# A two-stage conditioned MLP with layer norms: statistics first, GpSimd makes the norm's offset and the second table copies, z's transposes between the halves of a first layer

## The chip, the cores and the metric

The kernel runs on one core of a Trainium2 chip. The metric is the device time of one execution in microseconds; lower is better.

## The reference

Input `x` holds 128 sequences of 64 tokens with 256 features, with two numbers for each sequence: a condition (0, 1 or 2) and a domain (0 to 15).

```python
# stage 0, by condition
out_nr  = gelu(x @ w1_nr  + b1_nr)  @ w2_nr  + b2_nr      # two layers
out_tsr = gelu(x @ w1_tsr + b1_tsr) @ w2_tsr + b2_tsr     # two layers
out_sr  = gelu(gelu(x @ w1_sr + b1_sr) @ w2_sr + b2_sr) @ w3_sr + b3_sr   # three layers, 512 wide first
y = layernorm(x + chosen_out) * gamma + beta
# stage 1, by domain
h = gelu(y @ down_W.T + down_b)                           # 64 wide
h = h @ expert_W[domain].T + expert_b[domain] + domain_emb[domain]
out = layernorm(y + h @ up_W.T + up_b) * ln_gamma + ln_beta
```

All is float32. The gelu is exact.

## The kernel before

**Slots.** The kernel sorts the sequences by condition and packs four of one condition into a slot of 256 tokens: first the three-layer slots (`g < b_sr`), then the two-layer ones. A loop of steps runs over the slots, unrolled by two (parities p = 0 and 1, `q = 1 - p`). The first steps (HEAD) and the last (LAST2, LAST1, LAST0, DRAIN) are written out; the rest (MAIN) is a loop on each engine. Step g works on several slots at once: TensorE makes the last layer of slot g, the first layer of slot g + 1, the transposes of z of slot g - 1 and the expert products of slot g - 2; VectorE finishes slot g - 3.

**Precision.** A float32 product is made of three matmuls, high x high, low x high and high x low. ScalarE makes the high part (`x_hi`, L874; `h_hi`, L888), VectorE the low part of x (`x_lo`, L656), GpSimd the low part of h (`h_lo`, L478, `low()`).

**A two-layer step, engine by engine.** Each engine runs its instructions in the order written, and a wait on a semaphore stops all that stands behind it.

- TensorE: the last layer's products into ps_z (L1131 waits for H1's `h_hi`, then L1136 waits for H1's `h_lo`); the branch L1218; the first layer of the next slot, twelve products into H0 and H1 (L1060, waits for `x_lo`); a load of two register values with the places of the experts' tables (`tables_of`, L329); transposes of the normed z into ps_t (L1153, `zn`); the next slot's input added to ps_z (L1095, sets `x_used`); for slot g - 2 the residual and the expert products into ps_u (L1095, L1183); `down` into ps_d (L1196, waits for `yt`).
- ScalarE: gelu of H0 (high, then full), `yt` (L914, from ps_t), the cast `x_hi` of slot g + 2 (L874, waits for the load), gelu of H1, the adapter's gelu `stack` (L906), `zn` (L895).
- VectorE: statistics of z (L682), the centring of slot g - 3 (L718, `n`), moments (L689), variances (L694, `ve`), `x_lo` (L656), statistics of ps_u (L705, L712), `nm` (L698: minus mean times reciprocal deviation), the output (L749, L751, `o`), the bias added to x (L668), two copies of expert tables into `second_table` (L734) with a load of two register values.
- GpSimd: `h_lo` of H0, the power -0.5 of the variances (L485, `rs`), `h_lo` of H1, an indirect DMA that stores half of an output slot (L512).
- SP: four loads of x (L366, slot g + 3, wait for `x_used`) and two stores (L354); once in two steps a load of twelve register values (L329).

The products of L1183 read `second_table`, so step g needs the copies of slot g - 2. The input has two buffers.

## Time and profile before

| | |
|---|---|
| median of 3 runs | 272.14 us (272.11 to 273.24) |
| the profiled execution | 273.42 us |
| its span, first to last instruction | 271.6 us |
| busy: PE, DVE, ACT, POOL | 254.8, 204.8, 193.2, 149.5 us |
| mean granted TensorE clock | 0.98 |
| chain that ended last | PE 58%, SPq 15%, issue 9%, DVE 8% |

PE is TensorE, DVE VectorE, ACT ScalarE, POOL GpSimd, SP SyncE. A letter q behind an engine (SPq, PEldq) means its sequencer: DMA issues, register loads and branches, which are not counted as busy. L12 is line 12 of the kernel. Times are from the start of the span. The three-layer steps last until about 105 us, the two-layer steps from there to about 250. An idle time names in brackets what ended it.

### The profile page before, as it was taken

How to read it: one execution, taken by the hardware profiler on the slowest of the kernel's cores; microseconds unless marked ns; L12 is line 12 of the kernel's file. 1: busy time of each engine (PE TensorE's matmuls, PEld its weight loads, DVE VectorE, ACT ScalarE, POOL GpSimd, SP SyncE). 2: the span in 40 equal slices, each digit the busy share in tenths (PEclk: the TensorE clock that was granted, in tenths of full speed). 3: DMA queues.
4: the chain of work that ended last, by engine and by line, in shares of the span. 5: the costliest groups of instructions: out<-in, count | busy, mean ns of one | idle time of the engine just before them, and what ended most of it. 6: DMA issues, size and time to landing. Idle time of an engine off the chain costs nothing.

```text
span 271.6 us, 8356 instructions
## 1 busy us (share of the span) xinstructions
PE 254.8 (94%) x2118; PEld 224.6 (83%) x2119; DVE 204.8 (75%) x724; ACT 193.2 (71%) x446; POOL 149.5 (55%) x168
## 2 busy tenths in 40 slices
PE   7999999999999998899999999999999999999780
PEld 7798998998998987788888888888888888888460
DVE  6769553474674674898889888888898888888764
ACT  3578479669669666687878888887778888876520
POOL 3134474464674673765655656565655656568352
PEclk9999999999999999999999999999999999999777
DMA  6372011012022122024243423324242433332122
GB/s 181 100 261 64 9 41 42 12 34 58 29 51 72 35 48 69 27 77 97 68 107 85 107 68 87 84 70 101 68 115 77 103 75 80 87 88 68 39 75 80
DMA packets 44098, 20.63 MB, mean 76 GB/s; under 512 B 37782, under 2 KB 42348, under 8 KB 44077
## 3 DMA queue, kind: packets, MB, share of 16 engines
q1 hardware_dynamic: 41385, 15.18, 22.7%
q0 software_dynamic: 1536, 4.20, 4.5%
q10 hardware_dynamic: 1156, 1.00, 1.3%
q8 instruction: 10, 0.16, 0.3%
q14 instruction: 11, 0.09, 0.1%
HBM read 11.69 MB, written 8.65 MB: 75 GB/s over the span
## 4 chain that ended last, share of the span: by engine, by line
PE 58%; SPq 15%; issue 9%; DVE 8%; POOL 3%; ACT 3%; DMA 1%; DVEq 1%; ACTq 1%; POOLq 0%
PE ps_h L1060 15%; PE ps_z L1131 9%; SPq L366 7%; PE ps_u L1183 7%; PE ps_z L1136 4%; PE ps_t L1153 4%; SPq L329 4%; PE ps_z L1095 3%; PE ps_u L1095 3%; SPq L354 3%; PE ps_d L1196 3%; PE ps_t L1234 2%; POOL h_lo L478 2%; PE ps_t L1237 2%; PE ps_t L1235 2%
## 5 line engine op out<-in xcount | busy, mean ns | idle before, releaser
L478 POOL TENSOR_TENSOR h_lo<-h,h_hi 128x256 fp32r<-128x256 f32 (+1 forms) x75 | 70.3, 937 | 75.1 <-ACT h L888 74.3
L485 POOL TENSOR_TENSOR rs<-ve,minus_half 128x4 f32<-128x4 f32 (+1 forms) x38 | 41.2, 1084 | 30.9 <-DVE ve L694 30.7
L895 ACT ACTIVATE zn<-ps_z,nm,rs 128x256 f32<-128x256 f32 x66 | 33.7, 562 | 28.5 <-DVE nm L698 28.5
L888 ACT ACTIVATE h_hi<-ps_h,per_feature_sb 128x256 fp32r<-128x256 f32 x84 | 38.8, 495 | 16.6 <-PE ps_h L1060 14.3
L682 DVE BATCH_NORM_STATS2 st<-ps_z 128x6 f32<-128x256 f32 x66 | 24.9, 418 | 31.9 <-PE ps_z L1136 31.9
L914 ACT ACTIVATE yt<-ps_t,per_feature_sb 128x256 f32<-128x256 f32 x66 | 34.1, 574 | 8.0 <-PE ps_t L1153 8.0
L512 POOL DMA_INDIRECT out<-o,out_rows_now x32 | 34.3, 1071 | 8.0 <-issue 5.4
L888 ACT ACTIVATE h<-ps_h,per_feature_sb 128x256 f32<-128x256 f32 x84 | 38.7, 497 | 0.0
L1131 PE MATMUL ps_z<-last_hi,h_hi 128*128 (+1 forms) x132 | 36.2, 306 | 2.2 <-ACT h_hi L888 0.9
L1183 PE MATMUL ps_u<-tables,stack 65*64 x132 | 36.9, 403 | 0.0
L1183 PE MATMUL ps_u<-second_table,stack 65*64 65x256 f32 x132 | 36.9, 403 | 0.0
L1131 PE MATMUL ps_z<-last_lo,h_hi 128*128 (+1 forms) x132 | 33.1, 282 | 0.0
L656 DVE TENSOR_TENSOR x_lo<-x,x_hi 128x512 fp32r<-128x512 f32 x33 | 23.5, 712 | 11.7 <-ACT x_hi L874 11.7
L1131 PEld LDWEIGHTS ps_z<-last_hi,h_hi 128*128 128x128 f32 x132 | 24.8, 188 | 7.6 <-issue 7.6
L751 DVE SCALAR_TENSOR_TENSOR o<-n,rs,per_feature_sb 128x256 f32<-128x256 f32 x66 | 28.9, 477 | 0.6 <-DVE n L718 0.3
L718 DVE SCALAR_TENSOR_TENSOR n<-ps_u,mv,per_feature_sb 128x256 f32<-128x256 f32 x66 | 28.3, 469 | 0.0
L1060 PE MATMUL ps_h<-x_hi,w_two_hi 128*128 128x256 f32 x96 | 27.6, 288 | 0.0
L906 ACT ACTIVATE stack<-ps_d,per_feature_sb 64x128 f32<-64x128 f32 x66 | 24.0, 364 | 4.6 <-PE ps_d L1196 3.4
L705 DVE BATCH_NORM_STATS2 st<-ps_u 128x6 f32<-128x256 f32 x66 | 24.9, 419 | 2.8 <-PE ps_u L1183 2.8
L1060 PE MATMUL ps_h<-x_hi,w_two_lo 128*128 128x256 f32 x96 | 27.0, 281 | 0.0
L1060 PE MATMUL ps_h<-x_lo,w_two_hi 128*128 128x256 f32 x96 | 26.9, 280 | 0.0
L1183 PEld LDWEIGHTS ps_u<-tables,stack 65*64 65x64 f32 x132 | 15.8, 140 | 11.0 <-issue 6.4
(148 smaller groups left out, 643.1 us busy)
## 6 DMA issues: line engine op xcount, KB each, us to landing
x<-in_x_feat SPq DMA_DIRECT2D x130, 64.0 KB, 2.2
out<-o SPq DMA_DIRECT2D x65, 64.0 KB, 2.1
last_sb<-in_last_w SPq DMA_DIRECT2D x1, 768.0 KB, 4.8
w_sr_sb<-in_w_sr SPq DMA_DIRECT2D x1, 512.0 KB, 3.9
w_sr_sb<-in_w_sr ACTq DMA_DIRECT2D x1, 512.0 KB, 4.8
w_two_sb<-in_w_two SPq DMA_DIRECT2D x1, 512.0 KB, 5.5
out<-o,out_rows_now POOLq DMA_INDIRECT x32, 2.7
per_unit_sb<-in_per_unit SPq DMA_DIRECT2D x1, 268.1 KB
```

The source lines that it names most:

```text
L478: pool.tensor_tensor(dst, full, high.bitcast(F32), ALU.subtract).then_inc(ready, 1)
L485: pool.tensor_tensor(RS[p][:, norms, :], VE[p][:, norms, :], half_of_two[:, norms, :], ALU.pow).then_inc(rstd, 1)
L512: pool.indirect_dma_start(out_rows, row, O[p][:, 1, :], None).then_inc(sc_out[p], 16)
L682: dve.bn_stats(ST[0][p][:, t, :], ZP[p][:, t, :]).then_inc(stat[0], 1)
L718: ins = dve.scalar_tensor_tensor(out=N2[p][:, t, :], in0=UP[p][:, t, :], scalar=MV[step][:, 1, t, 0:1], in1=G2[:, 0, :], op0=ALU.subtract, ...
L751: dve.scalar_tensor_tensor(out=O[q][:, t, :], in0=N2[q][:, t, :], scalar=RS[p][:, 1, t:t + 1], in1=G2[:, 1, :], op0=ALU.mult, op1=ALU.add) ...
L888: ins = act.activation(dst[:, m, :], src[m], ACT.Gelu, bias=COL[:, bass.ds(col + m, 1)])
L895: ins = act.activation(ZN[:, t, :], ZP[p][:, t, :], ACT.Identity, bias=NM[p][:, t:t + 1], scale=RS[p][:, 0, t:t + 1])
L914: ins = act.activation(YT[q][:, c, :], TP[:, c, :], ACT.Identity, bias=COL[:, COL_BETA1 + c:COL_BETA1 + c + 1], scale=COL[:, COL_G1 + c:CO ...
L1060: ins = pe.matmul(out_ap, lhs[a], rhs[b], start=first and n == 0, stop=last and n == 2)
L1131: pe.matmul(ZP[p][:, t, :], h2h[:, c, t * P:(t + 1) * P], rows(half, c), start=False, stop=False)
L1183: ins = pe.matmul(UP[p][own, t, :], S[p][:, t, own], table, start=False, stop=(t == TT - 1))
```

## The change

- VectorE: in a common step the moments and variances follow the statistics of z at once, and the centring of slot g - 3 comes behind them. A new operation makes minus the mean (`NEG`). `nm` is gone from VectorE, and so are the copies of the second table. The output (`finish`) now stands before the statistics of ps_u.
- GpSimd: a multiplication of 128x2 after the power makes `nm`. In a two-layer step the power stands ahead of both `h_lo`. At the end of a step GpSimd copies the second tables of slot g - 1, with a load of two register values.
- ScalarE: in a two-layer step the cast `x_hi` comes right after H0's gelu, ahead of `yt` (behind it in the step in which three-layer slots end); `zn` comes before the adapter's gelu. The branches of a step are merged into one.
- TensorE: in a two-layer step z's transposes stand between the products of H0 and those of H1. The register load `tables_of` moves ahead of `start_two`, directly behind the last layer's products.

```diff
@@ GpSimd
+            def minus_mean(count, p):
+                pool.wait_ge(rstd, count)
+                pool.tensor_tensor(NM[p][:, :], NEG[p][:, :], RS[p][:, 0, :], ALU.mult).then_inc(nmr, 1)
...
                 elif where != HEAD or g >= 0:
                     power(g + 1, p, BOTH)
+                    minus_mean(g + 1, p)
...
+            def copy_second_tables(slot, q, where):
+                rows = values(pool, IDS[0:1, 0, bass.ds(slot * G + TT, TT)], (TE - 1) * H)
+                if where == HEAD and slot == 0:
+                    pool.wait_ge(s_ct_in, 16)
+                    pool.wait_ge(s_table_act, TABLES_OF_ACT)
+                    pool.wait_ge(s_table_dve, TABLES_OF_DVE)
+                if where != HEAD or slot >= 2:
+                    pool.wait_ge(u_ps, slot - 1)
+                for t in range(TT):
+                    ins = pool.tensor_copy(SECOND_TABLE[q][:, t, :], TABLES[:, bass.ds(rows[t], H)])
+                ins.then_inc(second_table, 1)
...
                 if where == DRAIN:
                     q = 1 - p
+                    copy_second_tables(g - 1, q, where)
...
                 with pool.Else():
+                    powers(g, i, p, where)
                     for slot in on_slot(g, -1, where):
                         low(h2l[:, 0, :], h2[:, 0, :], h2h[:, 0, :], h0_full, h0_lo, g + 1)
-                    powers(g, i, p, where)
...
                 if where != LAST1:
                     store(g, i, p, where)
+                for slot in on_slot(g, 1, where):
+                    copy_second_tables(slot, 1 - p, where)
@@ VectorE
             def variances(p, norms):
+                if norms != SECOND:
+                    dve.tensor_scalar(NEG[p][:, :], MV[p][:, 0, :, 0], -1.0, None, ALU.mult)
...
                 for slot in on_slot(g, 0, where):
                     first_stats(slot, p)
+                    first_moments(slot, p)
+                variances(p, BOTH)
                 for slot in on_slot(g, 3, where):
                     center(slot, q, p)
-                for slot in on_slot(g, 0, where):
-                    first_moments(slot, p)
-                variances(p, BOTH)
                 for slot in on_slot(g, -2, where):
                     input_low(slot, p)
+                for slot in on_slot(g, 3, where):
+                    finish(slot, i - 2 if p == 0 else i - 1, q, where)
                 (statistics of ps_u)
-                for slot in on_slot(g, 0, where):
-                    minus_mean(slot, p, where)
-                for slot in on_slot(g, 3, where):
-                    finish(slot, i - 2 if p == 0 else i - 1, q, where)
...
-                for slot in on_slot(g, 0, where):
-                    copy_second_tables(slot, p)
@@ ScalarE, a step whose next slot has two layers
                             first_of_two(False)
+                            next_input(g, i, p, where)
                             for slot in on_slot(g, 1, where):
                                 residual_norm(slot, q, where)
-                next_input(g, i, p, where)
+                    second_of_two()
+                    for slot in on_slot(g, 0, where):
+                        normalise(slot, p, where)
+                    for slot in on_slot(g, 1, where):
+                        adapter_gelu(slot, q)
@@ TensorE
-                start_two(g, 1 - p, where)
-                adapter(g, p, where)
+                at = [tables_of(slot) for slot in on_slot(g, 2, where)]
+                def transposes_of_z():
+                    for slot in on_slot(g, 1, where):
+                        transposes(slot, where)
+                start_two(g, 1 - p, where, transposes_of_z)
+                adapter(g, p, where, at)
...
             def start_two(g, q, where, between):
                 weights_ready(where, g + 1, "w1_two")
                 with pe.If(g + 1 < b_nr):
                     pe.wait_ge(x_lo, g + 2)
-                    first_layer_two(q, 0)
+                    first_layer_two(q, 0, 0)
+                    between()
+                    first_layer_two(q, 0, 1)
```

In LAST1 and LAST0 the copies and `nm` go from VectorE in the same way.

## Rows read from the trace of the kernel before

**Rows 1.** Stages: window, us, busy us of PE, PEld, DVE, ACT, POOL; clock, DMA share, GB/s.

```profile
84.70:94.90 10.20, 10.20 (x90) 9.46 (x89) 6.38 (x20) 7.50 (x20) 6.47 (x6) 1.00 0.21 52
170.20:182.33 12.13, 11.88 (x104) 10.46 (x104) 10.48 (x41) 9.73 (x22) 7.08 (x8) 1.00 0.34 87
254.00:261.00 7.00, 7.00 (x38) 4.92 (x38) 4.54 (x16) 3.74 (x8) 4.13 (x7) 0.51 0.14 39
```

**Rows 2.** Timeline of SP's queue: start, duration, line, operation.

```profile
158.07 2.88 SPq L366 DMA_DIRECT2D x<-in_x_feat  x4
...
182.33 2.88 SPq L366 DMA_DIRECT2D x<-in_x_feat  x4
...
186.93 2.85 SPq L366 DMA_DIRECT2D x<-in_x_feat  x4
...
230.87 2.88 SPq L366 DMA_DIRECT2D x<-in_x_feat  x4
```

**Rows 3.** Waits of SP's queue, 110 to 240: total, times, longest.

```profile
SPq L366 <- PE ps_z L1095: 6.1, 1, 6.1
```

**Rows 4.** Pieces of the chain that ended last: start, duration.

```profile
160.41 2.27 DMA x<-in_x_feat
...
162.70 0.05 ACT x_hi L874
...
206.79 1.25 PE ps_z L1131 x8
```

**Rows 5.** Timeline of ScalarE, two steps.

```profile
185.12 0.48 ACT L888 ACTIVATE h_hi<-ps_h,per_feature_sb 128x256 fp32r<-128x256 f32 x1 [0.55 <-PE ps_h L1060]
...
186.16 1.02 ACT L914 ACTIVATE yt<-ps_t,per_feature_sb 128x256 f32<-128x256 f32 x2 [0.20 <-PE ps_t L1153]
...
188.31 0.47 ACT L888 ACTIVATE h<-ps_h,per_feature_sb 128x256 f32<-128x256 f32 x1
...
204.40 1.02 ACT L914 ACTIVATE yt<-ps_t,per_feature_sb 128x256 f32<-128x256 f32 x2 [0.19 <-PE ps_t L1153]
205.32 0.61 ACT L874 CAST x_hi<-x 128x512 fp32r<-128x512 f32 x1
```

**Rows 6.** Timeline of TensorE, a two-layer step and the end.

```profile
184.10 0.28 PE L1060 MATMUL ps_h<-x_hi,w_two_hi 128*128 128x256 f32 x1
...
185.96 0.60 PE L1095 MATMUL ps_z<-ident,x 128*128 128x128 f32 x4
...
188.56 0.38 PE L1131 MATMUL ps_z<-last_hi,h_hi 128*128 x1
...
190.24 0.38 PE L1060 MATMUL ps_h<-x_hi,w_two_hi 128*128 128x256 f32 x1
...
253.25 0.66 PE L1153 MATMUL ps_t<-ident,zn 128*128 128x128 f32 x4 [2.03 <-ACT zn L895]
```

**Rows 7.** The page, part 5: L1060's products on w_two_hi.

```profile
L1060 PE MATMUL ps_h<-x_hi,w_two_hi 128*128 128x256 f32 x96 | 27.6, 288 | 0.0
```

**Rows 8.** Lines L1218, L329 on TensorE's queue: ns min/median/max, first and last start.

```profile
L1218 PEldq COMPARE_BRANCH  x1: 210/210/210, 189.6 to 189.6; - x1
...
L329 PEldq TENSOR_LOAD <-ids x5: 307/308/546, 182.0 to 194.2; - x5
```

**Rows 9.** Timelines of VectorE and GpSimd.

```profile
99.93 1.20 DVE L698 SCALAR_TENSOR_TENSOR nm<-mv,rs 128x2 f32<-128x2 f32 x1
...
99.84 1.28 POOL L478 TENSOR_TENSOR h_lo<-h,h_hi 128x512 fp32r<-128x512 f32 x1
...
188.85 0.74 POOL L478 TENSOR_TENSOR h_lo<-h,h_hi 128x256 fp32r<-128x256 f32 x1 [0.37 <-ACT h L888]
...
249.71 0.72 POOL L478 TENSOR_TENSOR h_lo<-h,h_hi 128x256 fp32r<-128x256 f32 x1
```

**Rows 10.** Groups of GpSimd by form: busy us, mean ns.

```profile
L503 POOL COPY out_rows_now<-out_rows 128x1 int32 x4 | 0.8, 201 | 0.0
```

**Rows 11.** Waits of TensorE, 14 to 60 us.

```profile
PE ps_z L1095 <- ACT zn L895: 0.4, 2, 0.2
```

More of the change, by code:

```diff
@@ L144, in conditioned_layers @@
         RS = [sb(f"rs{p}", [P, 2, TT]) for p in range(2)]
+        NEG = [sb(f"minus_mean{p}", [P, TT]) for p in range(2)]
         NM = [sb(f"nm{p}", [P, TT]) for p in range(2)]
@@ L728, in last_variances @@
                 variances(q, SECOND)
-            def copy_second_tables(slot, p):
-                rows = values(dve, IDS[0:1, 0, bass.ds(slot * G + TT, TT)], (TE - 1) * H)
-                for t in range(TT):
-                    ins = dve.tensor_copy(SECOND_TABLE[p][:, t, :], TABLES[:, bass.ds(rows[t], H)])
-                ins.then_inc(second_table, 1)
             def finish(slot, i, q, where, tiles=((1, o1_made), (0, o_made))):
@@ L835, in _ @@
                     add_bias(slot, p)
-                if where == HEAD and g == 0:
-                    dve.wait_ge(s_ct_in, 16)
-                    dve.wait_ge(s_table_act, TABLES_OF_ACT)
-                    dve.wait_ge(s_table_dve, TABLES_OF_DVE)
-                for slot in on_slot(g, 0, where):
-                    copy_second_tables(slot, p)
         @block.scalar
@@ L956, in first_of_two, with second_of_two @@
                         gelu(h2[:, 0:1, :], h2h[:, 0:1, :], [H0[:, 0, :]], first, h0_hi, h0_full)
+                def second_of_two():
+                    for slot in on_slot(g, -1, where):
+                        second = 2 * kind_of(act, slot) + 1
+                        act.wait_ge(h1_ps, g + 2)
+                        gelu(h2[:, 1:2, :], h2h[:, 1:2, :], [H1[:, 0, :]], second, h1_hi, h1_full)
                 with act.If(g + 1 < b_sr):
@@ L966, in _ @@
                         first_of_two(False)
+                        next_input(g, i, p, where)
                     else:
@@ L972, in _ @@
                             first_of_two(True)
+                            next_input(g, i, p, where)
                         with act.Else():
                             first_of_two(False)
+                            next_input(g, i, p, where)
                             for slot in on_slot(g, 1, where):
                                 residual_norm(slot, q, where)
-                next_input(g, i, p, where)
-                with act.If(g + 1 < b_sr):
-                    act.wait_ge(h1_ps, g + 2)
-                    gelu(h1[:, 2:4, :], h1h[:, 2:4, :], [H1[:, 0, :], H1[:, 1, :]], COL_B1_SR + 2, h1_hi, h1_full)
-                with act.Else():
-                    for slot in on_slot(g, -1, where):
-                        second = 2 * kind_of(act, slot) + 1
-                        act.wait_ge(h1_ps, g + 2)
-                        gelu(h2[:, 1:2, :], h2h[:, 1:2, :], [H1[:, 0, :]], second, h1_hi, h1_full)
+                    second_of_two()
+                    for slot in on_slot(g, 0, where):
+                        normalise(slot, p, where)
+                    for slot in on_slot(g, 1, where):
+                        adapter_gelu(slot, q)
                 if where == HEAD and g < 0:
@@ L1081, in first_layer_sr, with first_layer_two @@
                 ins.then_inc(ready, 1)
-            def first_layer_two(p, row):
-                for m, (bank, ready) in enumerate(((H0, h0_ps), (H1, h1_ps))):
-                    for c in range(KC):
-                        ins = products(bank[:, 0, :], weight("w1_two", row, H, c, m),
-                                       (flat(XH[p][:, c, :, :]), flat(XL[p][:, c, :, :])), c == 0, c == KC - 1)
-                    ins.then_inc(ready, 1)
+            def first_layer_two(p, row, m):
+                bank, ready = ((H0, h0_ps), (H1, h1_ps))[m]
+                for c in range(KC):
+                    ins = products(bank[:, 0, :], weight("w1_two", row, H, c, m),
+                                   (flat(XH[p][:, c, :, :]), flat(XL[p][:, c, :, :])), c == 0, c == KC - 1)
+                ins.then_inc(ready, 1)
             def residual(bank, source):
@@ L1198, in down, with adapter @@
                 ins.then_inc(d_ps, 1)
-            def adapter(g, p, where):
-                at = [tables_of(slot) for slot in on_slot(g, 2, where)]
-                for slot in on_slot(g, 1, where):
-                    transposes(slot, where)
+            def adapter(g, p, where, at):
                 input_residual(g, 1 - p, where)
@@ L1213, in start_sr, with start_two @@
                 first_layer_sr(q, half)
-            def start_two(g, q, where):
+            def start_two(g, q, where, between):
                 weights_ready(where, g + 1, "w1_two")
@@ L1223, in start_two @@
                         pe.wait_ge(x_lo, g + 2)
-                        first_layer_two(q, KC)
+                        first_layer_two(q, KC, 0)
+                    between()
+                    for slot in next_slot(g, q, where):
+                        first_layer_two(q, KC, 1)
             def middle_layer(g, half, highs):
@@ L1297, in _ @@
                     with pe.Else():
-                        start_two(g, q, where)
+                        start_two(g, q, where, lambda: None)
                 elif where == DRAIN:
```

23 lines of the change are left out of this document (6 added, 17 removed).

## The prediction

> **What bounds the kernel now.** I read the page first, then a table of stages, then SP's queue, because it takes so much of the chain. The page has TensorE busy for 94% of the span, which looks like a kernel bound by TensorE. For the three-layer steps that holds: 10.20 of 10.20 us [rows 1]. In the two-layer steps the chain runs along SP's queue and through the landing of a load. SP's times show why: its loads for every second step start at 158.07, 182.33 and 230.87 [rows 2], which is 72.80 / 6 = 12.13 us for two steps. SP's last wait in the stage is one of 6.1 us before all of these [rows 3]. A pair is four loads, two stores, four loads, two stores and a load of twelve register values. Nothing in the change touches that. **So the two-layer stage has a floor of 12.13 us a pair, and it already stands on it.** TensorE is just under it, with 11.88 of 12.13 busy [rows 1].
>
> The two are coupled by one load. The last DMA of the load begun at 158.07 starts at 160.41 and lands 2.27 us later, that is 4.61 after the first. ScalarE's cast x_hi starts at 162.70, in the same moment [rows 2, 4]. The load is just in time for a cast that stands behind yt.
>
> At the end TensorE waits 2.03 us for zn, until 253.25 [rows 6], and from 254 to 261 its clock is granted at 0.51, the 1.2 GHz level [rows 1].
>
> **The change in the two-layer step.** I count from a step's first L1060 product, 184.10 [rows 6].
>
> 1. The register load of the tables' places on TensorE's queue. It moves from behind the twelve L1060 products to ahead of them, behind the wait for h_lo. The queue really stands still there: GpSimd's h_lo ends at 188.85 + 0.74 = 189.59, the branch L1218 runs at 189.6, and L1060 starts at 190.24 [rows 6, 8, 9], 0.65 after h_lo. The load of two values takes 0.55 [rows 8], with its address 0.60, and it now stands in that gap. Before, the twelve products covered it. The Trainium skill (TensorE: Matmul & The Clock Gate, "Architectural detail") gives TensorE a queue of 64 instructions; by that the load would be hidden and cost nothing. The row of L1218, which sits right behind the end of h_lo, speaks against it.
>
> 2. ScalarE's order. H0's gelus start at +1.02 (185.12) and yt follows when the transposes are done, at +2.06 (186.16) [rows 5]. Now z's transposes come earlier and hide, but the cast stands ahead of yt. A gelu's 0.48 and the cast's 0.61 overlap the next operation by some 0.1 (204.40 + 1.02 = 205.42, but x_hi starts at 205.32), so yt starts at 1.02 + 0.37 + 0.37 + 0.51 = +2.27, 0.21 later. In the step after the loop's branch, L1131 starts at 206.79, 1.37 us after yt ends at 205.42 [rows 4, 5]: TensorE's queue runs branches and loads between, and L1131 moves one for one with yt. It comes at 2.27 + 1.02 + 1.37 = +4.66.
>
> 3. The other step. TensorE's own work puts L1131 at +4.46 (188.56). h_lo ends 1.28 after its gelu starts (188.31 to 189.59), so at 2.27 + 0.92 (yt) + 0.37 + 1.28 = +4.84, or 0.38 after L1131. With 0.65 and 0.60 behind it L1060 starts 1.63 after L1131. In the first kind of step TensorE's products reach from L1131 to L1060 in about 1.55 and cover the load. The pair by TensorE, its queue and ScalarE: 4.66 + 1.55 + 4.46 + 1.63 = 12.30 us.
>
> 4. The load of x. The cast wants its data at 1.02 + 0.74 = +1.76; before, behind yt, at 2.06 + 0.92 = +2.98. What it waits now delays yt, H1's gelu and h_lo in ScalarE's order. SP starts a load at most 0.97 after L1095's first product on z (185.96, then 186.93), that is at +2.83. The critical load is the next: 12.13 - (186.93 - 182.33) = 7.53 later [rows 2], landed after 4.61 more, at +14.97. It is wanted at T + 1.76, where T is the pair. The wait is 13.21 - T, and h_lo has no slack behind it, so T = 12.30 + 13.21 - T, T = 12.76. As 0.97 is an upper figure I take **12.7 us a pair, +0.57**.
>
> The 96 products of L1060 on w_two_hi are 24 two-layer steps [rows 7]. Without the first and the last two that is 10.5 pairs. **+6.0 us.**
>
> Bounds. With the table load hidden, point 3 has TensorE's own 1.5 in place of 1.63 and some 0.4 of slack for the wait, and T = 12.4 (+2.8 us). Nothing can give less than 12.13 (0). Above is contention: VectorE's tiny nm, begun at 99.93, takes 1.20 us while GpSimd's h_lo runs from 99.84 to 101.12 [rows 9]. The new order puts x_lo and both o beside GpSimd's mult and first h_lo. Half such a stall (an o or x_lo caught in front of H1's h_lo) gives about 0.5 a step: T = 13.1 to 13.2, +10.7 us. I take none, since H1's h_lo has room ahead of it on GpSimd: the power may start at +1.7, and 1.04, the mult and one h_lo of 0.74 end at about +3.8, against a start at +4.1.
>
> GpSimd's new work. Its mult of 128x2 lies between its copy of 128x1, 0.20 [rows 10], and the two-input 128x256 h_lo of 0.74; being almost as small as the first, I take 0.25. Its copies of 65x256 lie between the same two rows; by size they are near the second and have one input instead of two: 0.45 each. With 0.55 for the register values this is 1.7 us a step beside 7.08 / 2 = 3.5 busy [rows 1]: 5.2 of 6.06. It hides beside TensorE's step, and costs nothing while the copies end before the next variances. At 0.74 a copy it is 5.8 and the next power is late, which is rival C again.
>
> VectorE loses nm, the copies and their register load, and gains one 128x2 operation. Its variances come earlier, without the centring in front. This gives cover that the stage can't use: zn was ready before z's transposes, and is so even with them 0.7 earlier, since TensorE shows no wait for it there.
>
> **Elsewhere.** Three-layer steps: the mult delays the second h_lo of 1.28 by 0.25, under 10.2 us of products without a gap; 0. First steps: TensorE waits for zn, 0.4 us in all [rows 11], behind a stalled nm; **-0.4**. The end: GpSimd now does its power, mult and both h_lo in a row. The first h_lo (0.73) and the mult (0.25) come in front of the second, which ends at 249.71 + 0.72 + 0.98 = 251.4 [rows 9]. L1136 ends 0.65 later and z's transposes start at 252.1 instead of 253.25: -1.15. GpSimd's copies ahead of its last stores and powers give some 0.35 back: **-0.8**. Bounds: 0 (h_lo later still) and -3.5 (also no low clock: seven us of products at half speed, of which the other engines hide more than half).
>
> Sum: 6.0 - 0.4 - 0.8 = +4.8. The profiled execution took 273.42, its span 271.6 and 1.8 around it, and would become 278.2. The runs' median, 272.14, becomes **276.9 us**.
>
> **Rivals.**
> A. Faster. The stage stays on SP's floor, T = 12.13, because the table load hides and the load of x lands before the cast wants it. Only the ends count: 272.14 - 1.2 = 270.9, and 268.5 if the clock isn't lowered. For it: SP's pace is exact and the same in all six pairs. Against: the row of L1218, and data that lands at about +3.0 and is wanted at +1.8. It decides below T = 12.15. Chance 0.17.
> B. No change. T = 12.2 to 12.3: 0.7 to 1.8, which the ends give back, 272.3. For it: the slack of 0.4 if the table load hides. Against: the same landing. Chance 0.18.
> C. The shared port. H1's h_lo is caught behind o or x_lo, T near 13.1: 272.14 + 10.2 - 1.2 = 281.1. For it: the nm row. Against: the room in front of H1's h_lo. The Trainium skill (SBUF — State Buffer, "SBUF: two separate sides") has VectorE operations with two SBUF inputs and GpSimd exclude each other for a whole instruction; the row of nm agrees, as it ends when h_lo does. Chance 0.14.
> D. The forecast, T from 12.45 to 12.95: 274.3 to 279.5. Chance 0.51.
>
> **The numbers.** Likeliest 276.9, its own range 274.3 to 279.5. To hold 8 in 10 the range takes in B, the upper part of A and the lower part of C: 270.3 to 280.6. A measurement of this kernel tells about 0.5%, 1.4 us, from no change. Faster: most of A, 0.16. Same: the rest of A, B and the bottom of D, 0.21. Slower: D and C, 0.63.
>
> **What would show it.** In the profile after: x_hi ahead of yt, with a wait for the load in one step of two; yt 2.2 us or more after the first L1060; TensorE's register load between h_lo's end and L1218, and L1060 at least 1.6 after L1131 in that step; SP, which never waited in the stage, waiting for L1095 once a pair; pairs of 12.7 us. I am wrong if SP still waits for nothing from 121 to 236: then it is A or B. If H1's h_lo starts later than 0.1 us after its gelu's end, it is C. At the end the wait for zn should fall below 0.5 us.

## The result and the profile after

The changed kernel takes 284.19 us (median of 4 runs, 283.78 to 284.57), the kernel before beside it 272.12 (270.97 to 273.24). The ratio is 1.044, 95% interval 1.040 to 1.049: slower by 12.1 us. I had forecast 276.9 in a range of 270.3 to 280.6. The direction was right and the size was not.

The page, parts 1 and 4, of the changed kernel:

```profile
PE 256.7 (91%) x2118; PEld 224.1 (79%) x2119; DVE 216.0 (76%) x657; ACT 186.5 (66%) x446; POOL 183.0 (65%) x268
...
DVE 36%; issue 18%; POOL 12%; PE 7%; DVEq 3%; DMA 1%; POOLq 1%
```

Its span is 282.9 us. Before, the chain was 58% TensorE and 15% SP's queue; TensorE is down to 7% and SP's queue is gone. VectorE has 67 instructions fewer (657 against 724) and is busy for 11 us more (216.0 against 204.8). So single operations of it have become longer. These do it (part 5 of the page: count, busy us, mean ns), where before `o` took 477 ns in the mean and the bias 370:

```profile
L766 DVE SCALAR_TENSOR_TENSOR o<-n,rs,per_feature_sb 128x256 f32<-128x256 f32 x66 | 52.4, 832 | 3.2 <-POOL rs L486 2.8
...
L693 DVE TENSOR_SCALAR x<-x,slot_bias 128x256 f32<-128x256 f32 x66 | 30.1, 496 | 0.1
```

One two-layer step on VectorE's timeline (start, duration):

```profile
188.41 0.87 DVE L740 SCALAR_TENSOR_TENSOR n<-ps_u,mv,per_feature_sb 128x256 f32<-128x256 f32 x2
189.19 0.68 DVE L681 TENSOR_TENSOR x_lo<-x,x_hi 128x512 fp32r<-128x512 f32 x1
...
190.02 1.75 DVE L766 SCALAR_TENSOR_TENSOR o<-n,rs,per_feature_sb 128x256 f32<-128x256 f32 x2
191.69 0.75 DVE L727 BATCH_NORM_STATS2 st<-ps_u 128x6 f32<-128x256 f32 x2
192.58 0.25 DVE L734 BATCH_NORM_AGGREGATE mv<-st 128x2 f32<-128x6 f32 x2
192.77 0.93 DVE L693 TENSOR_SCALAR x<-x,slot_bias 128x256 f32<-128x256 f32 x2
193.62 0.75 DVE L707 BATCH_NORM_STATS2 st<-ps_z 128x6 f32<-128x256 f32 x2
```

and GpSimd's at the same time:

```profile
188.59 1.05 POOL L486 TENSOR_TENSOR rs<-ve,minus_half 128x4 f32<-128x4 f32 x1 [1.59 <-DVE ve L721]
189.71 0.22 POOL L492 TENSOR_TENSOR nm<-minus_mean,rs 128x2 f32<-128x2 f32 x1
189.88 1.60 POOL L479 TENSOR_TENSOR h_lo<-h,h_hi 128x256 fp32r<-128x256 f32 x2
191.66 1.06 POOL L534 DMA_INDIRECT out<-o,out_rows_now  x1 [0.17 <-issue]
192.73 0.82 POOL L517 COPY second_table<-tables 65x256 f32 x2
195.13 1.05 POOL L486 TENSOR_TENSOR rs<-ve,minus_half 128x4 f32<-128x4 f32 x1 [1.58 <-DVE ve L721]
```

Three things are to be seen. VectorE's list has hardly any idle time in it: none of these rows names a releaser, and from 121 to 250 us VectorE waits for no other engine. GpSimd, in contrast, waits 1.59 us in every step for VectorE's variances, so its own list is not what sets the step. Its power starts every 6.54 us (188.59, 195.13). The two `o`, 0.87 us before, take 1.75 and lie beside the two h_lo of 1.60. The bias (two operations, 0.61 before) takes 0.93 and lies beside GpSimd's copies. One by one, the four operations of the two engines are:

```profile
189.88 0.73 POOL L479 TENSOR_TENSOR h_lo<-h,h_hi 128x256 fp32r<-128x256 f32 x1
190.02 0.88 DVE L766 SCALAR_TENSOR_TENSOR o<-n,rs,per_feature_sb 128x256 f32<-128x256 f32 x1
190.57 0.91 POOL L479 TENSOR_TENSOR h_lo<-h,h_hi 128x256 fp32r<-128x256 f32 x1
190.82 0.95 DVE L766 SCALAR_TENSOR_TENSOR o<-n,rs,per_feature_sb 128x256 f32<-128x256 f32 x1
```

Only the h_lo that starts first keeps its length of before (0.73). Each of the others starts while an operation of the other engine is under way, and is longer than alone (0.48 for an `o`, 0.73 for an h_lo). SP's loads, which had set the pace before [rows 2], now wait for L1101: 9.7 us in 10 waits from 118 to 250 us.

The stage now goes like this (windows; us, busy us of PE, PEld, DVE, ACT, POOL, then the clock), against 12.13 a pair [rows 1]:

```profile
183.98:197.07 13.09, 12.23 (x105) 10.56 (x105) 12.15 (x37) 9.03 (x23) 9.40 (x15) 1.00 0.32 79
```

Where the time lies, by the first last-layer product of a step: the three-layer steps and the first steps end 1.67 us later (106.74 against 105.07), the transition costs 0.80 more (118.28 against 115.81), and the 22 two-layer steps up to 262.47, against 249.01, add 10.99, or 1.00 a pair. The rest of the program is 2.2 us shorter (20.4 us against 22.6). Together +11.3 us of span. (That the 2.2 us at the end come from the change is not shown; see the last experiment.) TensorE's timeline, after and then before:

```profile
106.74 0.36 PE L1137 MATMUL ps_z<-last_hi,h_hi 128*128 128x256 f32 x1
...
118.28 0.39 PE L1137 MATMUL ps_z<-last_hi,h_hi 128*128 x1
...
262.47 0.39 PE L1137 MATMUL ps_z<-last_hi,h_hi 128*128 x1
```

```profile
105.07 0.36 PE L1131 MATMUL ps_z<-last_hi,h_hi 128*128 128x256 f32 x1
...
115.81 0.39 PE L1131 MATMUL ps_z<-last_hi,h_hi 128*128 x1
...
249.01 0.39 PE L1131 MATMUL ps_z<-last_hi,h_hi 128*128 x1
```

Two of the steps that I had forecast are in the trace all the same: SP waits once a pair, and TensorE stands still at its register load. L1066 (L1060 before) waits 0.56 us for nothing but TensorE's own queue:

```profile
198.12 0.71 PE L1142 MATMUL ps_z<-last_hi,h_lo 128*128 x4
199.39 0.38 PE L1066 MATMUL ps_h<-x_hi,w_two_hi 128*128 128x256 f32 x1 [0.56 <-issue]
```

From 186 us on this is so once a pair; before that the pause is 0.18 to 0.22. The third step, a cast that waits for the load of x, is not in this trace. None of them can be what bounds the step, since VectorE never waits for them. The experiments ask what each is worth, and what makes VectorE's list long.

### The profile page after: what moved, and what is told of

Read it like the earlier page. It is cut to its first block, busy times and chain, and to the rows that moved or that the text cites. A ratio compares the mean times of both kernels' runs of the same rounds, so it can differ in the third digit from the quotient of the medians.

```text
span 282.9 us, 8361 instructions
## 1 busy us (share of the span) xinstructions
PE 256.7 (91%) x2118; PEld 224.1 (79%) x2119; DVE 216.0 (76%) x657; ACT 186.5 (66%) x446; POOL 183.0 (65%) x268
## 4 chain that ended last, share of the span: by engine, by line
DVE 36%; issue 18%; POOL 12%; PE 7%; DVEq 3%; DMA 1%; POOLq 1%
POOL rs L486 11%; DVE o L766 10%; DVE st L707 7%; DVE st L727 7%; DVE x L693 3%; PE ps_h L1066 3%; DVE mv L714 3%; DVE mv L734 2%; DVE ve L721 2%; PE ps_z L1137 2%; DVE out_rows_now L764 1%; DMA out<-o,out_rows_now 1%; PE ps_z L1101 1%; PE ps_z L1142 1%; PE ps_t L1159 1%
## 5 line engine op out<-in xcount | busy, mean ns | idle before, releaser
L479 POOL TENSOR_TENSOR h_lo<-h,h_hi 128x256 fp32r<-128x256 f32 (+1 forms) x75 | 74.0, 1000 | 30.9 <-ACT h L890 30.9
L486 POOL TENSOR_TENSOR rs<-ve,minus_half 128x4 f32<-128x4 f32 (+1 forms) x38 | 38.7, 1018 | 50.2 <-DVE ve L721 50.1
L766 DVE SCALAR_TENSOR_TENSOR o<-n,rs,per_feature_sb 128x256 f32<-128x256 f32 x66 | 52.4, 832 | 3.2 <-POOL rs L486 2.8
L1189 PE MATMUL ps_u<-tables,stack 65*64 x132 | 35.5, 392 | 0.5 <-POOL second_table L517 0.5
L1066 PE MATMUL ps_h<-x_hi,w_two_hi 128*128 128x256 f32 x96 | 31.3, 326 | 5.1 <-issue 4.7
L1189 PE MATMUL ps_u<-second_table,stack 65*64 65x256 f32 x132 | 35.6, 392 | 0.0
L693 DVE TENSOR_SCALAR x<-x,slot_bias 128x256 f32<-128x256 f32 x66 | 30.1, 496 | 0.1
L517 POOL COPY second_table<-tables 65x256 f32 x66 | 26.9, 437 | 0.4
L1066 PE MATMUL ps_h<-x_hi,w_two_lo 128*128 128x256 f32 x96 | 27.1, 282 | 0.0
L1066 PE MATMUL ps_h<-x_lo,w_two_hi 128*128 128x256 f32 x96 | 26.9, 280 | 0.0
L1066 PEld LDWEIGHTS ps_h<-x_hi,w_two_hi 128*128 128x128 f32 x96 | 18.1, 189 | 9.0 <-issue 8.5
```

The costliest lines, as they stand in the source:

```text
L479: pool.tensor_tensor(dst, full, high.bitcast(F32), ALU.subtract).then_inc(ready, 1)
L486: pool.tensor_tensor(RS[p][:, norms, :], VE[p][:, norms, :], half_of_two[:, norms, :], ALU.pow).then_inc(rstd, 1)
L693: ins = dve.tensor_scalar(XF[p][:, c, :, :], XF[p][:, c, :, :], SLOT_B[:, c, bass.ds(slot, 1)], None, ALU.add)
L766: dve.scalar_tensor_tensor(out=O[q][:, t, :], in0=N2[q][:, t, :], scalar=RS[p][:, 1, t:t + 1], in1=G2[:, 1, :], op0=ALU.mult, op1=ALU.add) ...
L1066: ins = pe.matmul(out_ap, lhs[a], rhs[b], start=first and n == 0, stop=last and n == 2)
L1189: ins = pe.matmul(UP[p][own, t, :], S[p][:, t, own], table, start=False, stop=(t == TT - 1))
```

## The experiments

The kernels ran in four groups, each on one chip together with the kernel before, whose median was 273.75, 272.8, 274.03 and 273.66 us in them (single runs 270.8 to 275.9). Of its 55 runs there, the 12 with a mean granted clock of 0.988 or more took 270.8 to 272.0 us and the other 43, at 0.984 or less, 272.4 to 275.9. The other kernels' runs lie within 1.5 us of each other, but for three (early load alone, cast first alone, copies behind the bias: 2.2 to 3.8). So a difference of 1 us between kernels of two groups says little; those on which the argument rests are 2.2 to 12.6 us. The ratios are to the kernel before of the same group. Beside the times I give the length of a pair of two-layer steps, counted over the same 22 steps as above; the clock at the end of the program does not touch it.

### One part undone, and one part alone

**The finish late again.** On the changed kernel, VectorE's list:

```
-                for slot in on_slot(g, 3, where):
-                    finish(slot, i - 2 if p == 0 else i - 1, q, where)
                 for slot in on_slot(g, 2, where):
                     ...
                         second_stats(slot, p)
                         second_moments(slot, p, q)
+                for slot in on_slot(g, 3, where):
+                    finish(slot, i - 2 if p == 0 else i - 1, q, where)
```

> The changed kernel with one part undone: VectorE finishes the output tiles (the two operations o) behind the ps_u statistics of the step, as before the change, and not ahead of them. Theory 1 (VectorE is the bound: its list runs without a pause, and it is stretched because the two o operations, 0.87 us each before and 1.75 us now, run beside GpSimd's two h_lo): o now starts later, when GpSimd's h_lo are partly over, so the stretch shrinks by 0.5 to 1.7 us a pair of steps, and the time falls to 272 to 279 us. Theory 2 (my forecast's causes, the table registers ahead of the first layer and the cast ahead of yt on the way to the next load of x, set the pair, and VectorE is only as busy because it waits in line): the time stays within 1.5 us of 284.

Measured: 280.18 us, 1.026 of the kernel before (1.020 to 1.033). The four microseconds are less than theory 1 said and more than theory 2 allowed. VectorE's timeline shows what came up in place of the list:

```profile
199.65 0.76 DVE L727 BATCH_NORM_STATS2 st<-ps_u 128x6 f32<-128x256 f32 x2 [0.78 <-PE ps_u L1189]
...
201.06 1.01 DVE L766 SCALAR_TENSOR_TENSOR o<-n,rs,per_feature_sb 128x256 f32<-128x256 f32 x2
```

The two `o` are short again (1.01; the 0.87 and 1.75 us are for two of them together, not for each as the expectation has it) and VectorE waits for TensorE. TensorE's side is a second bound, close behind the first.

**The power between the two h_lo again.**

```
                 with pool.Else():
-                    powers(g, i, p, where)
                     ... low(h2l[:, 0, :], ...)
+                    powers(g, i, p, where)
                     ... low(h2l[:, 1, :], ...)
```

> The changed kernel with one part undone: in a two-layer step GpSimd makes the power rs and the norm's offset nm between its two h_lo, as it made the power before, and not ahead of both. Theory 1 (VectorE and GpSimd hold each other up where two-input operations of VectorE meet GpSimd's): the two h_lo no longer lie side by side with both o; one o meets one h_lo and one meets the power, so the step keeps part of the stretch: 278 to 285 us. Theory 2 (the order of the queues ahead of the load of x): no change, 284 within 1.5 us, or slower, since rs is made later and the normalised row with it.

Measured: 281.3 us, 1.032 (1.025 to 1.039), as theory 1 had it; `o` falls from 832 to 687 ns in the mean.

**The copies on VectorE again.** The function copy_second_tables and its calls go back to where they were in the diff.

> The changed kernel with one part undone: the second table's two copies are made by VectorE again (0.20 us each) and not by GpSimd (0.44 us each, beside VectorE's bias, which takes 0.93 us there and 0.61 before). Theory 1 (VectorE's list is the bound): VectorE gets 0.40 us of copies a step back and loses 0.32 us of the bias's stretch: the time stays at 284 within 2 us. A theory in which GpSimd's list is the bound (it holds 0.87 us less a step then): 275 to 280 us. Theory 2 (queues ahead of the load of x): within 1.5 us of 284.

Measured: 303.0 us, 1.110 (1.103 to 1.117). No theory had that. The list explains it when the register load on its queue is counted. The timeline of VectorE:

```profile
202.71 0.62 DVE L677 TENSOR_SCALAR x<-x,slot_bias 128x256 f32<-128x256 f32 x2
203.89 0.49 DVE L740 COPY second_table<-tables 65x256 f32 x2 [0.56 <-issue]
204.30 0.75 DVE L691 BATCH_NORM_STATS2 st<-ps_z 128x6 f32<-128x256 f32 x2
```

From the start of the bias to that of the next statistics it is 1.59 us, against 0.85 in the changed kernel (192.77 to 193.62): the copies' starts are 0.41 apart from the statistics', and 0.56 is the load of the two register values, which I had left out. So a step is 0.74 longer by these rows, 7.3 us, and the steps took 7.4 (power to power, 205.82 to 213.21). What is added to this list is paid in full, as it should be where the list is the bound. GpSimd's list got shorter by its copies, and that won nothing. Why the same load hid in the kernel before I have not settled.

**The early load of the tables' numbers alone, on the kernel before.**

```
                 ... last_layer(kind, ..., p)
+                at = [tables_of(slot) for slot in on_slot(g, 2, where)]
                 start_two(g, 1 - p, where)
-                adapter(g, p, where)
+                adapter(g, p, where, at)
```

> The kernel before with one part of the change alone: in a two-layer step TensorE loads the two numbers of the tables ahead of the next step's first layer and not behind it. Theory 2 (my forecast's first step: +0.60 us on the way from h_lo to the first layer, which delays the load of x by as much wherever nothing covers it): slower by 3 to 6 us, 275 to 278 us, and SP waits for ps_z more. Theory 1 (that delay lies in the slack that the queue's floor of 12.13 us leaves, and it was VectorE that set the changed kernel's step): within 1.5 us of 272.1.

Measured: 280.17 us, 1.029 (1.019 to 1.039), above the range of theory 2. The four runs are two of 278.4 and two of 282.0. In the profiled one (278.4) the two-layer steps take 140.55 us against 133.20, 12.78 a pair against 12.11, which is 7.4 us. Its span is only 5.0 more than before, since its end is shorter (19.8 us against 22.6, see the last experiment). SP's loads start at 184.73 and 197.72, 12.99 a pair, after a first half with 12.5, and SP waits for ps_z ten times. Theory 2's step is real:

```profile
184.73 2.88 SPq L366 DMA_DIRECT2D x<-in_x_feat  x4
...
197.72 2.88 SPq L366 DMA_DIRECT2D x<-in_x_feat  x4
```

```profile
194.06 0.38 PE L1060 MATMUL ps_h<-x_hi,w_two_hi 128*128 128x256 f32 x1 [0.52 <-issue]
```

So theory 1's claim that this delay lies in slack was wrong. Both theories hold a true bound.

### Two bounds, one table

**The tables' numbers late again, in the changed kernel.** The line `at = ...` goes back behind start_two.

> The changed kernel with one part undone: in a two-layer step TensorE loads the tables' two numbers behind the next step's first layer again. Two bounds seem to lie close together in the changed kernel: TensorE's list with the early load (13.0 us a pair of steps in the second half of the run before this one that had it alone) and VectorE's list with the o operations beside h_lo (13.1). If so, this change alone leaves VectorE's bound: 282 to 285 us. If my forecast's step is the whole cause, about 6 us come back: 277 to 279 us.

Measured: 284.24 us, 1.042 (1.037 to 1.048): nothing comes back.

**Both undone.** The load late and the finish late.

> The changed kernel with both undone, the early load of the tables' numbers and the early finish. Two bounds close together: with both gone the time falls by more than the two alone together (4 us for the finish alone): 271 to 276 us. If something else of the change (the cast ahead of yt, z's transposes between the halves, GpSimd's copies beside VectorE's bias) is the larger cause: it stays over 277 us.

Measured: 277.48 us, 1.017 (1.013 to 1.022). That is more than the two alone together (6.7 us against 4.0 and 0), as two bounds have it. But the time is over 277, the sign for one more cause in the change.

**ScalarE's order back too.**

```
                             first_of_two(False)
-                            next_input(g, i, p, where)
                             for slot in on_slot(g, 1, where):
                                 residual_norm(slot, q, where)
+                            next_input(g, i, p, where)
```

> As the run with both undone, and ScalarE's order in the two-layer step put back too: yt ahead of the cast x_hi. What is left of the change is GpSimd's norm offset and copies, the power ahead of both h_lo, the statistics at once, z's transposes between the halves, and the end of the program. If the cast ahead of yt costs what I forecast (yt 0.21 us later in each step, on the way to ps_u and to the next load of x): 2 us under the run with both undone at most. If it lies under other work: the same within 1 us. Both: 269 to 275 us.

Measured: 274.05 us, 1.004 (1.001 to 1.007). The order of cast and yt is worth 3.4 us there, more than the 2 that I gave it at most: it is that cause. The reason is seen best where it is changed alone.

**The cast ahead of yt alone, on the kernel before.** The same swap the other way.

> The kernel before with one part of the change alone: in a two-layer step ScalarE casts x_hi ahead of yt. My forecast's step 2 made yt 0.21 us later a step by it, and a pair 0.2 to 0.4 longer: 274 to 277 us. From the two runs that differ in this alone (277.5 and 274.05) it is 3.4 us, since the cast waits up to 1.2 us for the load of x and holds yt: 275 to 277 us. If it lies under other work here: 272 within 1 us.

Measured: 277.32 us, 1.015 (1.011 to 1.019), 12.71 a pair; 0.3 above both ranges, and nearest to the one with the cast that waits. ScalarE's timeline:

```profile
202.82 0.62 ACT L874 CAST x_hi<-x 128x512 fp32r<-128x512 f32 x1 [0.62 <-DMA x<-in_x_feat]
203.35 1.01 ACT L914 ACTIVATE yt<-ps_t,per_feature_sb 128x256 f32<-128x256 f32 x2
```

The cast waits 0.62 us for the load, and yt, whose input is there (z's transposes end at 202.36), stands behind it. Such a wait comes once a pair, 6.1 us in all from 121 to 250. This is point 4 of my forecast.

**Both queue parts undone, the early finish kept.** The load late and yt first, on the changed kernel.

> The changed kernel with the two queue parts undone: the tables' numbers loaded late on TensorE, yt ahead of the cast on ScalarE. VectorE's early finish beside both h_lo stays. If VectorE's list alone makes the time: 282 to 285 us, and VectorE still without a pause at 13.1 us a pair. If the queue parts still count beside it: 277 to 281 us.

Measured: 284.01 us, 1.039 (1.033 to 1.046), 13.10 a pair. VectorE's list alone makes the whole time of the changed kernel, and the two `o` are as long as there:

```profile
202.84 1.76 DVE L766 SCALAR_TENSOR_TENSOR o<-n,rs,per_feature_sb 128x256 f32<-128x256 f32 x2
```

The medians in one table, the queue parts down and the finish across, with the length of a pair behind them:

| queue parts | finish early | finish late |
|---|---|---|
| both made (cast first, load early) | 284.19 (13.11) | 280.18 (12.93) |
| load late | 284.24 (13.09) | 277.48 (12.71) |
| load late and yt first | 284.01 (13.10) | 274.05 (12.39) |

The left column is flat: one bound, VectorE's. In the right column the same two parts are worth 2.7 and 3.4 us. And the place of the finish is worth 10.0 us once nothing else holds (284.01 to 274.05); 2.1 of these lie in the three-layer steps.

### Company or order

**h_lo short, in the changed kernel.** `low(h2l[:, 0, 0:32], ...)` and the same for the second; the low parts of the other 224 columns are left out.

> The changed kernel, in which GpSimd's two h_lo of a two-layer step make only 32 of their 256 columns (the low parts of the other columns are left out, so that the two-layer steps' last products take what stood in the buffer). It takes 0.6 us off each h_lo on TensorE's way and the company away from both o. If VectorE's stretch beside GpSimd is the cause: o falls from 0.83 to some 0.45 us in the mean and the time to 268 to 276 us. If VectorE's list would be as long without that company (its own work and waits): o may be short, but the time stays over 280 us.

Measured: 278.8 us, 1.022 (1.017 to 1.027). `o` falls to 550 ns, and the time ends between the two cases. The queue parts were still in, which left the question open, so:

**h_lo short, with both queue parts undone.** Again 32 of 256 columns; the rest of the low parts is left out.

> The same kernel, in which GpSimd's two h_lo of a two-layer step make only 32 of their 256 columns (the low parts of the others are left out). If the company of GpSimd makes VectorE's list long: o back at 0.87 us for two and not 1.75, and the time 269 to 274 us, 10 us or more under the run without it. If the order of the list makes it long: over 278 us.

Measured: 271.40 us, 0.994 (0.991 to 0.997), 12.6 us under the same kernel with whole h_lo. The list has the same order, `o` early:

```profile
200.68 0.77 DVE L681 TENSOR_TENSOR x_lo<-x,x_hi 128x512 fp32r<-128x512 f32 x1 [0.61 <-ACT x_hi L876]
...
201.62 0.87 DVE L766 SCALAR_TENSOR_TENSOR o<-n,rs,per_feature_sb 128x256 f32<-128x256 f32 x2
```

Two `o` in 0.87, and VectorE waits for ScalarE. A pair takes 12.04 us, and SP's queue is 38% of the chain: the steps are back on SP's floor. So it is the company that makes the list long and not its order. Shorter h_lo also spare TensorE a wait (0.44 us a step, 8.4 in all from 121 to 250, in the kernel with whole h_lo) and make GpSimd's list shorter. But the chain there is 7% TensorE against 36% VectorE, and GpSimd waits 1.6 us a step for VectorE, so I don't put the 12.6 us there.

**The early finish alone, on the kernel before.** `minus_mean` and `finish` go ahead of `second_stats`.

> The kernel before with VectorE's norm offset and finish ahead of the ps_u statistics, nothing else changed. GpSimd's list is that of before, h_lo, power, h_lo, so that o comes beside the second h_lo at most. If it is the order together with that company that costs in the changed kernel: o longer than 0.87 us for the two in most steps, and 273 to 280 us. If the order alone does nothing without the power's place: 272 within 1.5 us.

Measured: 318.23 us, 1.162 (1.159 to 1.165), far over the range. The company of `o` is not the cause here: `o` takes 489 ns in the mean against 477. One step of VectorE, and the power of GpSimd:

```profile
221.43 0.69 DVE L656 TENSOR_TENSOR x_lo<-x,x_hi 128x512 fp32r<-128x512 f32 x1
223.06 0.69 DVE L698 SCALAR_TENSOR_TENSOR nm<-mv,rs 128x2 f32<-128x2 f32 x1 [0.94 <-POOL rs L485]
...
223.73 0.87 DVE L751 SCALAR_TENSOR_TENSOR o<-n,rs,per_feature_sb 128x256 f32<-128x256 f32 x2
```

```profile
221.58 1.45 POOL L485 TENSOR_TENSOR rs<-ve,minus_half 128x4 f32<-128x4 f32 x1 [2.23 <-DVE ve L694]
```

nm waits 0.94 for the power and then takes 0.69 for 2 columns, beside the h_lo that GpSimd begins at 223.01 (0.71); all that VectorE has to do stands behind it, while VectorE's variances are what the power waited for. Over the 22 two-layer steps, which take 35.6 us more than before, VectorE waits 17.8 us for the power, nm takes 617 ns in the mean against 139 (10.5 us), the copies' register load costs 6.9 us, and the copies themselves, now beside an h_lo, 456 ns against 282 (7.7 us); 6.7 us of waiting for x_hi are saved. These sum to 36. I had priced the move by `o` alone and not asked what nm, which moves with it, waits for. In the changed kernel nm is GpSimd's, and this wait is not there.

### What is left, and what it is good for

**The copies behind the bias.** On the kernel with three parts back, GpSimd waits for the bias ahead of its copies: `pool.wait_ge(x_sum, g + 3)`.

> The run with three parts of the change put back (274.05 us), with one wait more: GpSimd starts its two copies only when VectorE has finished the bias of that step. In that run the bias took 1.20 us beside the copies, against 0.61 alone, and VectorE ran without a pause at 12.4 us a pair. If the company of the copies is what keeps it above the kernel before: the bias is back at 0.61, the pair goes to 12.1, and the time to 269 to 272 us. If the copies only move onto other work of VectorE, or come late for GpSimd's power: 273 to 276 us.

Measured: 275.31 us, 1.006 (1.003 to 1.010). The bias is down from 1.20 to 0.71, but nothing is won (12.41 a pair against 12.39):

```profile
204.87 0.76 POOL L517 COPY second_table<-tables 65x256 f32 x2 [0.92 <-issue]
205.71 1.05 POOL L486 TENSOR_TENSOR rs<-ve,minus_half 128x4 f32<-128x4 f32 x1
```

The copies' load of two register values stands behind the wait, costs 0.92 us there (0.90 to 1.25 in other steps), and the power comes right behind the copies without a pause.

**The load ahead of that wait.**

```
                 rows = values(pool, IDS[0:1, 0, bass.ds(slot * G + TT, TT)], (TE - 1) * H)
                 ...
+                pool.wait_ge(x_sum, slot + 4)
                 ...
                     ins = pool.tensor_copy(SECOND_TABLE[q][:, t, :], ...)
```

> As the run with the copies behind the bias (275.3 us), with GpSimd's load of the two table numbers ahead of that wait and not behind it. There the copies began 0.9 to 1.2 us after the bias's end with nothing but issue before them, and the power behind them came late. If that load was the price: the copies begin within 0.4 us of the bias's end and the time is 270 to 273 us. If the copies are too long for that place at any start: 274 to 276 us.

Measured: 271.88 us (12 runs, 271.65 to 273.15), 0.996 of the kernel before (0.9925 to 0.9999), 12.20 a pair.

```profile
203.73 0.74 POOL L519 COPY second_table<-tables 65x256 f32 x2 [1.03 <-DVE x L695]
204.99 1.04 POOL L486 TENSOR_TENSOR rs<-ve,minus_half 128x4 f32<-128x4 f32 x1 [0.52 <-DVE ve L723]
```

The copies follow the bias at once, the power has 0.5 us to spare, and SP waits for nothing from 118 to 235 us: the kernel is back on SP's floor but for one pair of 12.43 (12.18 in the mean over nine, 121.14 to 230.72). So GpSimd can take this work over without loss, and nothing shows that it wins anything by it.

**The end alone, on the kernel before.** In the last two steps GpSimd makes nm behind its power, from a negated mean that VectorE leaves.

> The kernel before with one part of the change alone, in the last two steps only: GpSimd makes the norm's offset nm right behind its power there, from a negated mean that VectorE leaves. In the kernel before TensorE waited 2.03 us for zn at 253.25 and its clock stood at 0.50 to 0.67 for the 8 us behind that. If that wait and that clock are where the changed kernel's end gains 2.2 us: 269.5 to 271.5 us. If the wait belongs to the order of VectorE's earlier work and not to the offset: 272 within 1 us.

Measured: 272.33 us, 0.994 (0.992 to 0.995) of the kernel before beside it (274.03). That is above the 269.5 to 271.5 expected, from a kernel before that was 1.9 us above its first median too. In its timeline and windows:

```profile
252.45 0.65 PE L1161 MATMUL ps_t<-ident,zn 128*128 128x128 f32 x4 [0.61 <-issue]
```

```profile
254.00:261.00 7.00, 5.93 (x54) 4.16 (x52) 5.36 (x19) 3.53 (x9) 4.13 (x7) 1.00 0.14 41
```

The wait of 2.03 us for zn [rows 6] is gone and so is the low clock of 0.51 [rows 1]. From the last two-layer step's first last-layer product (249.38) to the end (270.7) it is 21.3 us, against 22.6. But it is not shown that the wait brings the low clock. The kernel with the cast first alone keeps the last two steps as before. TensorE waits 1.62 us for zn in it, and yet the clock stays full until TensorE has finished; its clock row of the page stands here behind that of the kernel before:

```profile
259.46 0.66 PE L1156 MATMUL ps_t<-ident,zn 128*128 128x128 f32 x4 [1.62 <-ACT zn L895]
```

```profile
PEclk9999999999999999999999999999999999999777
PEclk9999999999999999999999999999999999999996
```

Its end takes 19.7 us. The kernel with the early load alone is the same case: it waits 1.97 us for zn, and its end takes 19.8. So the old end at full clock is no longer than the changed kernel's 20.4. What this kernel and the one with the load ahead of the wait have over the kernel before, 0.6 and 0.4% of its median, is therefore not shown to be a gain of their order: the 12 runs of the kernel before at a mean clock of 0.988 or more took 270.8 to 272.0 us, no longer than these two. Both beat the changed kernel by 12 us. The two were not made one.

## Why the prediction was wrong

**The step that failed** is the sentence on contention: "I take none, since H1's h_lo has room ahead of it on GpSimd", with the one on VectorE, whose earlier list "gives cover that the stage can't use". I had seen that "the new order puts x_lo and both o beside GpSimd's mult and first h_lo", and priced it only by what a late h_lo would do to TensorE. But a stall has two sides. GpSimd did have room. VectorE had not: its list is 6.54 us a step with the company. Without it, the two `o` are 0.88 shorter and the bias 0.32, which leaves 5.34. The floor was 12.13 / 2 = 6.06 [rows 2]. So 0.7 us of room stood against 1.2 us of stall. The length of the list could have been counted in the trace of before, and the stall bounded by the lengths of `o` and h_lo. With the length as it was measured, the term that I took as nothing is 22 steps of 6.54 - 6.06, or 10.6 us; the steps became 11.0 longer.

**Rival C** had the right neighbours, `o` beside h_lo, and its pair near 13.1 is what was measured (13.11), but it had the wrong victim. The sign that I gave for it, H1's h_lo more than 0.1 us after its gelu, did appear (h ends at 183.69 and the second h_lo starts at 184.01), and TensorE's waits from 121 to 250 do not name it. The sign was bound to the mechanism that I had in mind. "VectorE has no idle time left" would have been the sign of the one that acts.

The Trainium skill (SBUF — State Buffer, "SBUF: two separate sides") says that the pair of ports which VectorE and GpSimd share goes to whichever instruction starts first, for its whole length. The rows agree: the h_lo that starts at 189.88 keeps its 0.73, each of the three that follow has an operation of the other engine under way at its start, and all three are longer than alone. But the later one is not held in every case: x_lo starts at 189.19, while the power begun at 188.59 runs for 1.05, and takes its usual 0.68. Together two `o` take 0.87 alone and 1.75 beside two h_lo, which grow from 1.42 (two in a row in the version with three parts back) to 1.60. I had quoted that page for C, and drawn from it only what it does to GpSimd.

**Steps 1 to 4 were real, and hidden.** The load in front of L1060: forecast 1.25 us from h_lo's end to the first product, measured 1.35 (h_lo, begun at 196.43, ends 1.61 later at 198.04, and L1066 starts at 199.39). Alone it costs 7.4 us of the stage, 0.67 a pair. The Trainium skill (TensorE: Matmul & The Clock Gate, "Architectural detail") gives that engine a queue of 64. I read this as a queue in which the load would cost nothing, and this run speaks against that reading, as the row of L1218 did. The cast that waits for the load of x and holds yt: 0.62 us in the row above; alone it costs 0.60 a pair, where I had 12.4 - 12.13, or 0.27, for it. In the changed kernel itself the cast never waited. I had +0.57 a pair and +6.0 us for both together, and 280.18 - 274.05 = 6.1 us separates the two kernels that differ in just these. That this agrees is in part luck, since it is the way from 12.39 to 12.93 a pair and not from SP's floor of 12.13, and on the kernel before either part alone costs as much (0.67 and 0.60). No run has both there. And the terms of two bounds don't add, the longer one counts, and it was VectorE's.

**Three-layer steps, forecast 0, measured 1.7 us.** The same company: two `o` take 1.85 beside the h_lo of 128x512, the bias behind them is late, and TensorE waits for it, some 0.3 us a step. The last wait is longer, 1.67 us at 104.37, but there the kernel before waits 0.75 too (102.65).

```profile
90.17 1.85 DVE L766 SCALAR_TENSOR_TENSOR o<-n,rs,per_feature_sb 128x256 f32<-128x256 f32 x2
...
93.03 0.73 DVE L693 TENSOR_SCALAR x<-x,slot_bias 128x256 f32<-128x256 f32 x2
```

```profile
93.81 0.66 PE L1101 MATMUL ps_z<-ident,x 128*128 128x128 f32 x4 [0.27 <-DVE x L693]
```

With the finish late and all else alike (the two kernels of the table's last row) these steps end at 104.43 and not at 106.50. I had looked only at the mult in front of h_lo.

**The end, forecast -0.8 with -3.5 as the bound, measured -2.2.** The transposes of z come 2.64 us after the step's first last-layer product (262.47 to 265.11), and before 4.24 (249.01 to 253.25): 1.6 us gained where I had 1.15. But the clock is full from 264 to 274 us here and was at 0.51 in the profiled execution of the kernel before. With the old end at full clock it takes 19.7 and 19.8 us in the two kernels named above, so of the 2.2 us nothing is shown to come from the new order.

**GpSimd's new work** was sized well: copies of 437 ns against 450, the mult 219 against 250, and it hid. But the copies are the bias's company; that is worth 2.2 us in the version where it decides (274.05 against 271.88, ratios 1.001 to 1.007 and 0.9925 to 0.9999). Of the transition to two-layer steps (+0.80 us, 11.54 against 10.74) 0.44 is gone with the load late (11.10); the rest I have not traced to an instruction.

## What to carry to other kernels

When work moves to an idle engine or an operation moves in a list, write out who runs beside whom, and price each stall on both sides: the engine that has room absorbs it, the one whose list is nearly as long as the step does not. For every engine compare the length of its list with the floor of the stage, before and after, and count the stalls and register loads into the length. Where two lists come out close, undoing one part of a change can show nothing; undo them in pairs. And before a gain at the end is put down to the change, compare the granted clock there in both profiled executions.

## What the runs showed of the hardware

- The company of GpSimd also costs an operation with one SBUF input: two biases took 0.61 us alone and 1.20 in the kernel with three parts back, where they lie beside the end of GpSimd's store and the two copies of 65x256; with the copies moved away it was 0.71.
- It works the other way too, and who starts first decides: the power `rs` of 128x4 took 1.45 us where x_lo had begun 0.15 us before it (in 20 of the 23 powers from 113 us on in the run with the early finish alone, and at 108.77 in the kernel before), and 1.04 or 1.05 where x_lo began behind it (0.09 us or more in the kernel before, 0.6 in the changed one).
- What a load of two register values costs depends on its place. On TensorE, behind the wait for h_lo, it left a pause of 0.50 to 0.56 us once a pair in the second half of the stage, and of 0.15 to 0.24 in the first half. In VectorE's list of the run with the copies back it was 0.44 to 0.61, and on GpSimd behind the wait for the bias 0.90 to 1.25. Moved ahead of that wait on GpSimd, it vanished, and the kernel gained 3.4 us.
